# The first half of batch 0's attention scores inside the end of a gated convolution

## What is computed

```
# 1. gated convolution
xi, gate = split(x @ w_in.T)                       # 1024 channels each
h = silu(causal_conv(xi, 4 taps) + conv_b) * D * silu(gate);   part = h @ w_out.T
# 2. cross attention, 16 heads of 32, on a context of 8 x 256 x 128
q = x @ Wq.T;   k, v = split(ctx @ Wkv_expand.T)
attn = softmax(where(causal, q k^T / sqrt(32), -big));   part = (attn @ v) @ Wout.T
# 3. shared expert plus the top 2 of 8 routed experts
```

## Time and profile before

| | |
|---|---|
| median of 3 runs | 1034.68 us (1033.60 to 1035.37) |
| the profiled execution | 1032.64 us, its span 1030.9 us |
| PE busy (PE's weight loads) | 974.0 us, 94% (832.1 us, 81%) |
| VectorE, ScalarE, POOL busy | 680.8, 528.5, 257.0 us |
| granted PE clock, mean | 0.978 of full speed |
| convolution's block | 0 to 288 us |
| attention's block | 288 to 522 us |
| batch 0's attend begins | 333.62 us |

### The profile page before, as it was taken

The page is one execution under the profiler, slowest core; times in us unless marked ns, Lnnn a source line. Parts: engine busy times, 40 slices in busy tenths (PEclk is TensorE's granted clock), DMA queues, the critical chain, the costliest instruction groups (busy, mean ns, idle before and its releaser), DMA issues. The chain is left out here.

```text
span 1030.9 us, 17414 instructions
## 1 busy us (share of the span) xinstructions
PE 974.0 (94%) x5776; PEld 832.1 (81%) x5776; DVE 680.8 (66%) x1554; ACT 528.5 (51%) x1264; POOL 257.0 (25%) x373
## 2 busy tenths in 40 slices
PE   7999999999978999998889979999999998999996
PEld 6888888888867888887668769898999897878785
DVE  5946556378267888886477657767777775254576
ACT  5624414236269888899653146655665664121120
POOL 3430110102133333334430022222222120603040
PEclk9999999999996999999899999999999999899999
DMA  4223023021795999986720278878778881705041
GB/s 165 102 102 122 0 75 139 0 82 64 232 217 144 266 227 257 269 223 169 271 89 21 104 240 262 261 253 279 266 243 258 270 278 59 233 11 203 1 174 71
DMA packets 87758, 172.74 MB, mean 168 GB/s; under 512 B 8624, under 2 KB 36528, under 8 KB 85904
## 3 DMA queue, kind: packets, MB, share of 16 engines
q1 hardware_dynamic: 80560, 149.95, 46.9%
q0 software_dynamic: 7136, 22.03, 6.5%
HBM read 131.05 MB, written 37.49 MB: 163 GB/s over the span
## 5 line engine op out<-in xcount | busy, mean ns | idle before, releaser
L804 ACT ACTIVATE b_dump<-b_dump,b_peak 128x128 f32<-128x128 f32 (+1 forms) x256 | 113.3, 446 | 6.3 <-DVE b_peak L938 6.0
L45 PE MATMUL e_ps_h<-e_x_lo,e_gu_hi 128*128 128x256 f32 (+1 forms) x384 | 110.5, 288 | 2.8 <-DVE e_x_lo L2159 1.3
L45 PE MATMUL a_ps_proj<-region_a_rounded,arena 128*128 128x512 f32 x272 | 107.2, 394 | 6.3 <-DVE region_a_rounded L368 6.3
L46 PE MATMUL e_ps_h<-e_x_hi,e_gu_lo 128*128 128x256 f32 (+1 forms) x384 | 107.5, 280 | 0.0
L47 PE MATMUL e_ps_h<-e_x_hi,e_gu_hi 128*128 128x256 f32 (+1 forms) x384 | 107.4, 280 | 0.0
L46 PE MATMUL a_ps_proj<-region_a_rounded,arena 128*128 128x512 f32 x272 | 106.8, 393 | 0.0
L47 PE MATMUL a_ps_proj<-region_a_rounded,arena 128*128 128x512 f32 x272 | 106.8, 393 | 0.0
L387 DVE SCALAR_TENSOR_TENSOR f_region_b<-a_ps_proj,a_taps,f_region_b 128x510 f32<-128x510 f32 (+2 forms) x96 | 71.7, 747 | 37.9 <-ACT f_region_b L328 35.5
L938 DVE CUSTOM_DVE_ANT_0 b_dump<-b_ps_s,b_mask 128x128 f32<-128x128 f32 (+1 forms) x256 | 80.0, 352 | 21.5 <-PE b_ps_s L1139 18.4
L2165 DVE TENSOR_TENSOR e_gu_lo<-f_region_a,e_gu_hi 128x704 fp32r<-128x704 f32 x92 | 81.3, 887 | 14.9 <-ACT e_gu_hi L2071 14.3
L2071 ACT ACTIVATE e_gu_hi<-f_region_a 128x704 fp32r<-128x704 f32 x92 | 71.8, 784 | 23.9 <-PEq L1475 15.2
(11 more groups left out here) (407 smaller groups left out, 2667.5 us busy)
## 6 DMA issues: line engine op xcount, KB each, us to landing
f_region_a<-we_gate_up SPq DMA_DIRECT2D x88, 352.0 KB, 5.2
qk_split<-arena SPq DMA_DIRECT2D x24, 512.0 KB, 5.3
y_slots<-f_region_b SPq DMA_DIRECT2D x16, 512.0 KB, 3.8
f_x_next<-x SPq DMA_DIRECT2D x6, 1024.0 KB, 8.2
b_sk<-qk_split SPq DMA_DIRECT2D x24, 256.0 KB, 4.5
b_sq<-qk_split SPq DMA_DIRECT2D x24, 256.0 KB, 6.1
f_region_a<-we_down SPq DMA_DIRECT2D x12, 512.0 KB, 4.3
f_region_b<-we_down SPq DMA_DIRECT2D x11, 512.0 KB, 4.2
```

The costliest lines, as they stand in the source:

```text
L45: pe.matmul(out, a_hi, b_lo, start=first, stop=False)
L46: pe.matmul(out, a_lo, b_hi, start=False, stop=False)
L804: ins = act.activation(dump[:, n % DUMPS, cols], dump[:, n % DUMPS, cols], ACT.Exp, scale=-1.0, bias=peak[:, u, k, i:i + 1], accum_out=tot ...
```

## The change

- The softmax's tiles and semaphores, and the functions for one head (`score`, `least`, `add_up`, `log`, `turn`, `row_hi`, `row_lo`, `lower`), move into a class `Softmax` that both blocks use.
- The first eight heads of batch 0 (`EARLY`) are scored in the convolution's block: PE makes one score behind each of the output's steps 14 to 21 of the last 24, VectorE and ScalarE their maxima and sums, and behind the last step their shifted peaks are turned, cut, and stored by POOL's DMA into the query stack. ScalarE's table for exponent and logarithm is loaded there.
- The stacks of batch 0 are moved by three queues (SyncE, ScalarE, POOL) in another order, before `store_ahead`. The tiles `k_hi` and so on are laid out by batch, and a stack's heads in the order (h c), so that one run is 2 KB where it was 1 KB.
- Batch 1's stacks of the first half are loaded in the convolution's block, into the space of `wo_hi` and `wo_lo`, whose first chunks are read no more.
- POOL makes the mask at the kernel's start, and the rows of ones of batch 0's stack in the convolution's block.
- The attention's start-up part keeps the second half of batch 0, its values (now copied by VectorE) and the turning of batch 2. Keys and queries of batch 2 are made in turn 0: `projected(t)` is `t + 2`.

```diff
-        wo_hi = sb("a_wo_hi", [P, JC, D], F32R)
-        wo_lo = sb("a_wo_lo", [P, JC, D], F32R)
+        next_sq, next_sk = following_stacks
+        wo_hi, wo_lo = (x.rearrange("p u i t -> p (u i t)").rearrange("p (j d) -> p j d", j=JC) for x in (next_sk, next_sq))
...
+            stack_ahead(sp, first_sk, 0, k_hi, first_stacked)
+            stack_ahead(sp, first_sk, 2, k_hi, first_stacked)
+            sp.wait_ge(ahead_lo_done, 1 + 3 * DC)
+            sp.wait_ge(ahead_ready, 3 * DC)
+            stack_ahead(sp, first_sq, 0, q_lo, first_stacked)
             store_ahead(0, k_hi)
             store_ahead(1, k_lo)
-            for r, tile in enumerate((k_hi, k_lo, k_hi)):
-                stack_ahead(sp, first_sk, r, tile)
-            sp.wait_ge(ahead_lo_done, 1 + 3 * DC)
-            sp.wait_ge(ahead_ready, 3 * DC)
             store_ahead(2, q_hi)
             store_ahead(3, q_lo)
-            for r, tile in enumerate((q_lo, q_hi, q_hi)):
-                stack_ahead(sp, first_sq, r, tile)
-            sp.wait_ge(ahead_stored, 16 * (6 * HC + 8))
+            sp.wait_ge(ahead_stored, 16 * 8)
+            sp.wait_ge(s_ready, 1)
+            for into, parts in ((next_sk, (0, 1, 0)), (next_sq, (3, 2, 2))):
+                for r, kind in enumerate(parts):
+                    sp.dma_start(into[r * HD:(r + 1) * HD, 0].rearrange("p (h c) t -> p h (c t)", h=HC).bitcast(F32),
+                                 split_dram[1, 0, kind].rearrange("(h r) n -> r h n", h=HC).bitcast(F32))\
+                        .then_inc(soft.stack_loaded[0], 16)
...
+            stack_ahead(pool, first_sk, 1, k_lo, pool_moved)
+            pool.memset(rounded[1][K_ROWS:M_ROWS].bitcast(F32), 1.0)
+            pool.wait_ge(ahead_hi_done, 1 + 3 * DC)
+            pool.wait_ge(ahead_ready, 3 * DC)
+            stack_ahead(pool, first_sq, 1, q_hi, pool_moved)
+            pool.wait_ge(soft.m_lo_done, 1)
+            for r, m in ((K_ROWS, m_hi), (K_ROWS + 1, m_lo)):
+                pool.dma_start(rounded[0][r:r + 1, 0:UH * S].rearrange("p (i t) -> p i t", i=UH).bitcast(F32), m.bitcast(F32))\
+                    .then_inc(soft.m_loaded, 16)
...
+            stack_ahead(act, first_sq, 2, q_hi, first_stacked)
+            act.preload_act_table_set("natural_log_exp_and_others")
+            for n in range(EARLY):
+                act.wait_ge(max_done, n + 1)
+                soft.add_up(act, dump, n).then_inc(total_done, 1)
+                if n == UH - 1:
+                    act.wait_ge(total_done, UH)
+                    soft.log(act, 0).then_inc(log_done, 1)
+            act.wait_ge(soft.m_ready, 1)
+            soft.row_hi(act, m_hi, rows).then_inc(soft.m_hi_done, 1)
...
-            add_x(GROUPS - 1, x1)
+            dve.wait_ge(consts, 3)
+            for n in range(EARLY):
+                maxima(n)
+            dve.wait_ge(log_done, 1)
+            soft.lower(dve, 0).then_inc(soft.shift_done, 1)
+            add_x(LAST, x1, [0, 1, 2])
+            dve.wait_ge(ahead_stored, 16 * 8)
+            dve.wait_ge(soft.m_hi_done, 1)
+            soft.row_lo(dve, m_hi, m_lo, rows).then_inc(soft.m_lo_done, 1)
+            add_x(LAST, x1, [3])
...
+                        if scored <= j * TILES + t < scored + EARLY:
+                            score(j * TILES + t - scored)
+                        if end == JC and scored < JC * TILES and j * TILES + t == JC * TILES - 1:
+                            pe.wait_ge(soft.shift_done, 1)
+                            pe.wait_ge(ahead_stored, 16 * 8)
+                            soft.turn(pe, rows, ident[:], 0).then_inc(soft.m_ready, 1)
...
         def projected(t):
-            return {-1: GB, 0: B}.get(t, t + 2)
+            return t + 2
...
             for i in range(UH):
-                scores(0, 0, i)
+                scores(0, 1, i)
                 if i < BT:
                     value(0, 1 - i)
-                if i == 2:
+                if i == 3:
                     turn(GB, 0)
                     turn(GB, 1)
-                if i == 3:
-                    keys(GB, 0)
-                if i in (5, 7):
-                    query(GB, (i - 5) // 2)
-            for i in range(UH):
-                scores(0, 1, i)
-                if i == 0:
-                    keys(GB, 1)
-                if i == 1:
-                    peaks(0, 0)
-                if i in (2, 4):
-                    query(GB, UC + (i - 2) // 2)
```

More of the change, by code:

```diff
@@ L273, in _ @@
             pool.memset(ln.power[:], -0.5).then_inc(ln_const, 1)
+            pool.memset(soft.mask[:], 0.0).then_inc(consts, 1)
+            pool.wait_ge(consts, 1)
+            for c in (0, 2):
+                pool.affine_select(out=soft.mask[:, c * P:(c + 1) * P], in_=soft.mask[:, c * P:(c + 1) * P],
+                                   compare_op=ALU.is_ge, fill=MASKED, base=0, pattern=[[-1, P]], channel_multiplier=1)\
+                    .then_inc(consts, 1)
             def split_w(u):
@@ L396, in conv, with add_x, maxima @@
                 h_rest(g, JC - 1)
-            def add_x(g, into):
+            def add_x(g, into, tiles=range(TILES)):
                 dve.wait_ge(xt_loaded, 16 * g + 16)
-                for t in range(TILES):
+                for t in tiles:
                     dve.wait_ge(out_done, TILES * g + t + 1)
                     dve.tensor_tensor(into[:, t], ps_out[:, t], xt[:, t], ALU.add).then_inc(out_free, 1)
+            def maxima(n):
+                if n >= DUMPS:
+                    dve.wait_ge(total_done, n - DUMPS + 1)
+                dve.wait_ge(s_ready, n + 1)
+                soft.least(dve, dump, ps_proj[:, 1, n % 2], n).then_inc(max_done, 1)
             with dve.Fori(0, GROUPS - 1) as g:
@@ L439, in project, with score, output @@
                     mm.then_inc(proj_done, 1)
-            def output(g, first, end):
+            def score(n):
+                if n == 0:
+                    pe.wait_ge(ahead_lo_done, 1 + 3 * DC)
+                    pe.wait_ge(first_stacked, 16 * 4 * HC)
+                    pe.wait_ge(pool_moved, 16 * 2 * HC)
+                if n >= 2:
+                    pe.wait_ge(max_done, n - 1)
+                q, k = (r[0:K_ROWS, n * S:(n + 1) * S] for r in rounded)
+                soft.score(pe, ps_proj[:, 1, n % 2], q, k).then_inc(s_ready, 1)
+            def output(g, first, end, scored=JC * TILES):
                 pe.wait_ge(out_free, TILES * g)
@@ L687, in load_res @@
                 sp.dma_start(half(res, b), rows_of(x1_dram, b)).then_inc(res_loaded, 16)
[L689 to L691 removed]
+            load_stack(1, 1)
+            for t in range(END_T):
                 b = projected(t)
@@ L1137, in scores @@
                 q, k = (s[b % 2][0:K_ROWS, u, i] for s in (sq, sk))
-                for r in range(BT):
-                    mm = pe.matmul(ps_s[:, n % 2, r * P:(1 + 2 * r) * P], q[:, r * P:(r + 1) * P], k[:, 0:(r + 1) * P],
-                                   start=True, stop=True)
-                mm.then_inc(s_ready, 1)
+                soft.score(pe, ps_s[:, n % 2], q, k).then_inc(s_ready, 1)
             def peaks(b, u):
```

269 lines of the change are left out of this document (149 added, 120 removed).

## The result

The changed kernel takes 1036.01 us (median of 17 runs, 1033.87 to 1042.01) where the kernel before takes 1034.33 (17 runs beside them): ratio 1.0028, 95% interval 1.0017 to 1.0039. It is slower, by 2.9 us after the ratio (1.8 to 4.0; the two medians alone are 1.7 us apart), where 5.4 us of gain were forecast. The profiled execution of the changed kernel lasts 1035.23 us, with a span of 1033.6; that of before 1032.64, with 1030.9.

What follows compares the result with a forecast made beforehand. Only the seam between convolution and attention was taken to have time to find: small waits, then ACT, later turns at PE's pace. Terms -5.2 - 0.5 + 14.2 - 2.6 - 0.5 gave 5.4 us gained: 1029.3 us, range 1026.0 to 1033.0.

Steps and rivals of the forecast that it cites:

- early heads on PE, tail, issue of the rows, barrier, stacks' wait: Convolution's end: eight early scores and the rows delay the attention block by 5.2 us; waiting for stacks adds 0.5.
- the clock's term: Batch 0's turn: PE arrives at a lowered clock and its dense fill restores it; 0.5 us lost, range 0 to 2.5.
- The block's start: Attention block starts 0.3 us after its slowest engine, POOL, ends at 293.0: at 293.3 instead of 288.1 us.
- The stacks: First early score at 280.0 us waits for batch 0's stack transfers: 0.5 us, with 0 and 3 as ends.
- (b): Stacks come late, PE waits 3 us or more at score 0: 1031.8, or 1034 with 5 us; chance 0.12.
- The 2 us that I would have added by the rule: Stack loads: if three queues bring nothing once transfers bind, the whole forecast is some 2 us later.
- The short start and turn 0: Start-up: first exponent after 10.9 us, 14.2 gained; batch 0's turn bound by DVE at 23.0 us, 2.6 lost.
- The mark: Everything counted to batch 0's attend on PE, 333.62 us before; what follows is unchanged and runs at PE's pace.
- attends at other than 27.1 us: Sign of a wrong forecast: the stacks' new order matters in every batch, which was costed at nothing.
- (c): Early heads gain nothing: PE's waits for ACT and the longer tail eat the start's gain; about 1034.5, chance 0.06.
- (a): ACT stays the bound of batch 0's turn and DVE hides in its gaps: 1026.2, chance 0.12.
- (d): PE's clock stays about 0.5 through batch 0's turn, deciding below a mean of 0.61: slower, 1041, chance 0.06.

Runs made afterwards that it cites:

- e6: The changed kernel with a 128-byte gap ahead of a_h_hi and a_h_lo and POOL's two row transfers issued first in the attention block; ratio to before 0.9990.
- e7: The changed kernel with both corrections (128-byte gap, row transfers first in the attention block) plus useless matmuls in the start-up and turn 0; ratio 0.9988.
- e2: The changed kernel with an unused gap of 128 bytes ahead of a_h_hi and a_h_lo; ratio to before 1.0016.
- e1: The kernel before with an unused gap of 2432 bytes per partition, placing a_h_hi and a_h_lo where the changed kernel has them; ratio 1.0014.
- e4: The kernel before with only batch 2's keys and queries moved from the start-up into turn 0, all 16 heads kept in the start-up; ratio 1.0004.
- e3: The changed kernel with POOL's two row transfers issued first in the attention block instead of last in the convolution's; ratio 0.9995.
- e13: The changed kernel with both corrections, useless matmuls in start-up and turn 0, and batch 4's input and context loaded behind the residuals; 1031.13 us, ratio 0.9973.
- e16: The changed kernel with both corrections and batch 4's input and context loaded behind the residuals, without useless matmuls; 1031.77 us, ratio 0.9973.

## Why the prediction was wrong, step by step

Forecast and measured, in the changed kernel:

| step | forecast | measured |
|---|---|---|
| pace of the convolution's outputs | no term | 1.7 us late |
| early heads on PE, tail, issue of the rows, barrier, stacks' wait | 5.2 + 0.5 | 6.1 |
| POOL's drain behind the issue | no term (0.3 us for the barrier) | 2.3 us |
| block's first score to first exponent | 10.9 | 12.1 |
| first exponent to attend, with the clock's term | 23.0 + 0.5 | 24.8 |
| attend of batch 0 | 328.2 | 335.2 |
| the turn behind it | 27.1 | 27.4; 27.7 in e6, 29.5 in e7 |

**The block's start** is the step that failed: "with the same 0.3 us the new block starts at 293.3". It started at 298.27, and the 10.14 us of delay are 1.73 of pace (e2), 2.29 of POOL's drain behind the end of its issue (295.64 to 297.93), and 6.1 for all that I had priced at 5.7. That e6 starts it at 293.40, next to the forecast, is luck: it has neither of the two unpriced costs, but it doesn't have the issue of the rows in this block either, which I had priced at 1.7 us with its start. I had the row for POOL's issue and took its end for POOL's end. In the kernel before the convolution's block ends with no transfer of POOL's, so no row had this price; I should have bounded it from above by the landing of such rows (2.5 us from the issue, in the trace of before) instead of taking the barrier of a block that ends with DVE.

**The pace** was in no rival. I had excluded the convolution because its instructions don't change, but the tiles that they read were moved. It is 1.7 us at the block's start. At batch 0's attend it is 1.9 us in e1 and 1.2 in e2.

**The stacks** were sized right: 0.48 us of waiting, 0.5 forecast; rival (b) fell. Score 0 came late, at 282.56, so this alone could be luck, but e6, with the old pace, has it at 280.65 and waits 0.62 us. Where the earlier trace rows shows 2.8 us to landing, the changed kernel's transfers take 4.1 to 5.7, with a DMA share of 0.99 and 280 GB/s in 277 to 282.5 us, where the earlier trace rows has 0.98 and 296 GB/s with one queue. The Trainium skill, "DMA: Bandwidth & Descriptors", section "Issuing engines are not separate DMA queues", says that transfers of several issuing engines run interleaved on the same DMA engines, and the trace agrees: three queues move no more per second than one. The 2 us that I would have added by the rule didn't come.

**The short start and turn 0** were short in size by 1.2 and 1.3 us. DVE works 21.5 us in the turn where I had 23.0, so it isn't the bound by itself. At full clock the turn does take 22.9 us (e7), but no run shows that DVE sets it: it is busy 21.3 of them, PE 21.9 with the useless matmuls, and that this meets my 23.0 is in part luck. The mis-sized term is the clock, 0.5 us, which measures at 2.2 in turn 0 and 0.6 in the start-up (e6 against e7). My range for it in the turn, 0 to 2.5, held that part; for the start-up I had no such term. I had assumed that PE's fill brings the clock back and that it then stays; it came back at 312 to 314 us and fell again at 320 and 330, in the two places where a later turn has the output projection and turn 0 has nothing. Two busy times by stretch of the changed kernel:

```profile
314.00:316.00 2.00, 2.00 (x19) 2.00 (x18) 1.61 (x7) 1.72 (x8) 0.47 (x2) 1.00 0.67 255
...
320.00:322.00 2.00, 2.00 (x11) 2.00 (x11) 1.37 (x13) 1.14 (x5) 0.19 (x1) 0.50 0.91 289
```

The rule cited for it, the Trainium skill's "TensorE: Matmul & The Clock Gate", section "Why this matters for your kernels", spoke against the change, and the trace agrees with it: behind the idle 5.78 us the clock is 0.50, and with the gaps filled (e7) it is at 1.00 from 300 us on.

**The mark** was the last mistake. I counted everything to batch 0's attend, "since what comes behind it ... isn't changed and runs at PE's pace". The turn behind it takes 27.4 us in the changed kernel, and more where batch 0 is earlier. e7 reached 329.07 and had 2.15 of its 4.55 us left at the next attend. The prediction took attends at other than 27.1 us for a sign of the stacks' new order; but e4, which has the old one, takes 27.7 us for turn 1, as e6 does. So even with each term right, the forecast of 5.4 us would have been worth less: the projection in turn 0 puts batch 2's stacks, the normalised rows' store and the residuals into one stretch of full transfers.

**The rivals.** What came is closest to (c), which said that the early heads gain nothing: e4 against the changed kernel shows that, 8.2 us against 8.0. But it named PE's waits for ACT, two microseconds at each of three handoffs, and it was the pace, a drain and a clock; its time of 1034.5 was 1.5 too low, and by its own terms, three times two microseconds on 1029.3, it should have been 1035.3. (a) and (d) fell: ACT had 20.5 of 24.8 us, and the clock of turn 0 was 0.82, above the 0.61 below which (d) decides. Two slips in the working changed nothing: the key stack's transfers start at 265.8 us, not at 263, and four pairs of 0.69 and 0.69 us are 5.5, not 5.4.

## What to carry to other kernels

A step that becomes the last of a block is priced with what the block's end waits for, the drain of the engine that issued a transfer included; put such a transfer first in the next block. When a change adds or moves a small tile, look whether the tiles behind it keep their place, and compare the pace of matmuls that the change doesn't touch. And what is won at one mark counts only as far as the transfers behind it leave room: ask which load is next late before counting it to the end.

## What the runs showed of the hardware

- The same matmuls (128x512, stationary tiles `a_h_hi` and `a_h_lo`) followed at 228.9 ns with these tiles 64 bytes behind a multiple of 256 in each partition, at 232.4 with them on a multiple, at 233.4 with 192 bytes behind one. Of what they read, nothing else was moved.
- POOL's drain at the end of a block took 2.73 us behind two small transfers of rows that it had issued, 2.3 of them after the issue was over, and 0.97 us without them (e3); the next block began 3.5 us earlier when they were issued in it.
- PE's granted clock fell and rose several times within one start-up and turn (0.50 at 306 to 312, 320 to 322 and 330 to 332 us, up to 1.00 between), and useless matmuls in the thin places kept it at 1.00 from 300 us on (e7). The 2.8 us that this gained in the trace (e13 against e16, at batch 1's attend) can't be seen in the total times, whose intervals are about as wide.
- The same kernel had its clock at half for 3 to 4 us of batch 6's turn in one execution and for 7 in another; the turn took 24.3 and 25.8 us.
